# Opening of a deformable-convolution kernel: first table in quarters over six PSUM banks, last rows normalised first, patches of image 0 sent ahead of image 1's pixels

## The chip, the cores and the metric

One core of one Trainium2 chip runs the program. The metric is the device time in microseconds of one execution. The kernel before was run three times; the median is 560.41 us. The change alters only what happens in roughly the first third of the program; the rest is the same code.

## The reference, cut to what matters

The input x is 2 images of 32 channels, 64 x 64. Two residual layers follow each other, each on a group-normalised x (32 groups of one channel, so mean and variance of every channel of every image over its 4096 pixels).

```python
x = x + L0(gn(x))     # layer 0
x = x + L1(gn(x))     # layer 1

# layer 0: 3x3 convolution -> 4 offsets (dx, dy) and 4 logits per pixel
offsets = conv2d(v, offset_w, offset_b); attn = softmax(conv2d(v, weight_w, weight_b), axis=1)
sampled = grid_sample_border(v, gx + dx_n, gy + dy_n)     # 4 bilinear samples per pixel
y = conv2d(einsum('bkhwd,bkhw->bdhw', sampled, attn), proj_w)      # 1x1
y = batchnorm(y) over both images; return gelu(y)

# layer 1: 3x3 convolution -> 9 offset pairs and 9 gates, 9 bilinear samples, 3x3 output weights
```

## The kernel before, in words

All loops that concern us are in layer 0. A *group* is 512 pixels (8 image rows); each image has 8 groups, each group 4 *tiles* of 128 pixels. Layer 0 has two ways of sampling:

- **Gathers (kind "G").** Groups 0 to 4 of image 0, 20 tiles. `table00` is a DRAM table with one row of 128 floats per pixel: the 32 channels of the pixel and of its right, lower and lower right neighbour. GpSimd (POOL) issues four indirect DMAs per tile (line 565) that fetch one table row for every sample; DVE multiplies them by corner weights (line 1766, `prod`), and TensorE sums and turns the products (line 1003). There are four slots (`got`), so the gathers of tile k wait until DVE has used tile k-4 (semaphore `used`). They also wait for the whole table (`tab_out["00"]`) and for the indices of their group.
- **Windows (kind "W").** The other 11 groups, 44 tiles. `positions0` and `positions1` are DRAM copies of the raw images, pixel by pixel. A window DMA (line 490, `load_window`, two halves of 440 KB) brings 5 x 5 neighbourhoods for a group into one of two buffers in `shared`; DVE multiplies by 25 tap weights (line 1758, `samples`), TensorE sums them (line 1018). Window 0 and 1 are loaded before the loop.

The work is ordered by hand: each engine has its own list of instructions, and they meet at semaphores.

The opening. SyncE (SP) loads image 0 (four copies of the raw pixels, one for each corner shift: `x_first` for copy 0, `x_rest` for copies 1 to 3), copy 0 of image 1 and the constants `later`. DVE takes statistics; the scale and shift of each channel (`aff`) go through TensorE (line 1038) to all four partition groups. ACT and DVE normalise image 0 into `xn` by the table `SHARES` (lines 648 and 1366). TensorE makes the corner table by transposes (`make_corners`, line 926) in halves of 16 blocks, 4 corner banks each; ACT copies each bank to `trow` (line 665) and SP sends each half (line 473). `used_before` says which earlier use of a PSUM bank has to be copied away first. `make_pixels` (line 938) turns the raw pixels into patches (`prow`) for the window table; ACT copies them (line 722), SP sends them (line 479). The convolutions 0 to 15 (line 959) give offsets and logits for the items `G0, W0, G1, G2, W1, W2, G3, ...`; ACT copies each result to `conv_out` (line 677), and `turn_item` (line 996) brings it to pixel-by-row form for DVE. An item W1 needs convolution 5, W2 needs 6 and 7; from convolution 6 on image 1 is convolved.

The loop. STEPS = 20 steps m, one gather tile and two or three windows each. Tables say at which m TensorE turns an item (`TURN_AT`) and starts a convolution (`CONV_AT`), and when ACT normalises which part of image 1 (`NORM_AT`; eight pieces of 32 rows, the first before the loop). The bias of the 1x1 convolution is folded with image shifts (line 1078, y_bias line 743, `scale_fold` line 1788) before the loop, which needs `later`.

After the loop: batch statistics (line 1339), GELU, layer 1.

## Time and profile before

| | |
|---|---|
| three runs | 558.91, 560.41, 657.77 us; median 560.41 |
| profiled execution | 560.44 us, of which the span (first to last instruction) 558.6 us |
| busy share of the span | PE 83%, DVE 76%, POOL 68%, ACT 37% |
| mean granted TensorE clock | 0.90 of full speed |
| layer 0 up to the batch statistics | 0 to 168.4 us |
| layer 1 and what leads to it | 168.4 to 558.6 us |

In the rows, a time is in us from the start of the span; PE is TensorE, PEld its weight load, POOL is GpSimd, a q behind an engine marks its queue (DMA issues). In brackets stands how long the engine was idle before the row and what ended it. A TensorE instruction in 32-bit floats shows as two records (x8 for four matmuls).

### The profile page before, as it was taken

How to read it: one execution, taken by the hardware profiler on the slowest of the kernel's cores; microseconds unless marked ns; L12 is line 12 of the kernel's file. 1: busy time of each engine (PE TensorE's matmuls, PEld its weight loads, DVE VectorE, ACT ScalarE, POOL GpSimd, SP SyncE). 2: the span in 40 equal slices, each digit the busy share in tenths (PEclk: the TensorE clock that was granted, in tenths of full speed). 3: DMA queues.
4: the chain of work that ended last, by engine and by line, in shares of the span. 5: the costliest groups of instructions: out<-in, count | busy, mean ns of one | idle time of the engine just before them, and what ended most of it. 6: DMA issues, size and time to landing. Idle time of an engine off the chain costs nothing.

```text
span 558.6 us, 10900 instructions
## 1 busy us (share of the span) xinstructions
PE 464.5 (83%) x3923; PEld 263.8 (47%) x3923; DVE 422.2 (76%) x931; ACT 205.6 (37%) x342; POOL 379.2 (68%) x356
## 2 busy tenths in 40 slices
PE   5975589987870476989999999999898999998784
PEld 2545266665650332345556455555444544544443
DVE  4965529898767965678897898989788788788582
ACT  1813446322227557653433433333232332232211
POOL 5067635778744746576787777777777777777772
PEclk9855769999876576989999999999998999999999
DMA  9688443778710292111222224711112112111111
GB/s 198 192 201 198 116 93 59 162 144 137 159 30 2 76 176 61 38 62 48 73 90 73 71 91 90 102 55 53 53 48 57 53 48 58 58 53 57 54 53 30
DMA packets 42813, 48.48 MB, mean 87 GB/s; under 512 B 24454, under 2 KB 33926, under 8 KB 42000
## 3 DMA queue, kind: packets, MB, share of 16 engines
q1 hardware_dynamic: 31868, 25.52, 21.9%
q0 software_dynamic: 10752, 22.04, 14.8%
q8 instruction: 34, 0.56, 0.4%
q10 hardware_dynamic: 144, 0.24, 0.2%
q14 instruction: 15, 0.12, 0.1%
HBM read 39.02 MB, written 8.75 MB: 86 GB/s over the span
## 4 chain that ended last, share of the span: by engine, by line
PE 35%; POOL 25%; issue 15%; DMA 9%; DVE 7%; ACT 7%; SPq 1%; POOLq 1%; DVEq 0%; ACTq 0%
POOL got L565 23%; PE ps_later L1157 4%; PE ps_pair L1157 4%; PE ps_raw L1133 4%; PE ps_x L1170 4%; DMA shared<-positions 3%; ACT xn L648 3%; DMA got<-table,idx 3%; DVE samples L1758 2%; PE ps_x L1018 2%; PE ps_x L1180 2%; PE ps_raw L959 2%; PE ps_raw L1045 2%; PE ps_o L972 2%; DMA positions<-prow 2%
## 5 line engine op out<-in xcount | busy, mean ns | idle before, releaser
L565 POOL DMA_INDIRECT got<-table,idx x336 | 352.7, 1050 | 152.3 <-issue 106.9
L1775 DVE TENSOR_TENSOR prod<-got,wgt 128x512 f32<-128x512 f32 x64 | 44.3, 692 | 31.8 <-DMA got<-table,idx 31.2
L1576 DVE TENSOR_TENSOR vprod<-ps_pair,rhat 128x704 f32<-128x704 f32 x64 | 56.8, 887 | 9.2 <-PE ps_pair L1157 8.8
L1576 DVE TENSOR_TENSOR vprod<-ps_later,rhat 128x704 f32<-128x704 f32 x64 | 56.4, 882 | 1.9 <-PE ps_later L1157 1.9
L1758 DVE TENSOR_TENSOR samples<-shared,vprod 128x800 f32<-128x800 f32 x44 | 42.9, 981 | 18.4 <-DMA shared<-positions 8.7
L1170 PE MATMUL ps_x<-early,vprod 128*128 128x128 f32 x384 | 55.7, 281 | 0.8 <-DVE vprod L1584 0.5
L1170 PEld LDWEIGHTS ps_x<-early,vprod 128*128 128x128 f32 x384 | 41.9, 144 | 30.1 <-issue 16.1
L1584 DVE TENSOR_TENSOR vprod<-vprod 128x640 f32<-128x640 f32 x64 | 52.8, 824 | 1.2
L648 ACT ACTIVATE xn<-raw,aff 32x2048 f32<-32x2048 f32 (+4 forms) x20 | 42.6, 2139 | 12.5 <-DVE aff L1358 11.1
L1180 PE MATMUL ps_x<-early,prod 128*128 128x128 f32 x256 | 39.1, 275 | 9.5 <-DVE prod L1775 9.3
L1133 PE MATMUL ps_raw<-conv_out,later 128*128 128x512 f32 x64 | 40.6, 720 | 0.7 <-ACT shared L812 0.7
L798 ACT ACTIVATE samples<-ps_x 128x384 f32<-128x384 f32 x32 | 15.7, 490 | 63.4 <-PE ps_x L1180 60.3
L1018 PE MATMUL ps_x<-early,samples 128*128 128x128 f32 (+1 forms) x168 | 26.9, 320 | 13.0 <-DVE samples L1758 13.0
L1157 PE MATMUL ps_later<-y,shared 64*64 64x352 f32 x320 | 34.5, 503 | 1.9 <-DVE vprod L1576 0.7
L1157 PE MATMUL ps_pair<-y,shared 64*64 64x352 f32 x320 | 33.4, 488 | 2.6 <-DVE vprod L1576 1.5
L1180 PEld LDWEIGHTS ps_x<-early,prod 128*128 128x128 f32 x256 | 29.3, 141 | 12.2 <-DVE prod L1775 11.9
L1157 PE MATMUL ps_later<-y 64*64 64x352 f32 x320 | 32.8, 480 | 2.3 <-DVE vprod L1576 1.6
L1157 PE MATMUL ps_pair<-y 64*64 64x352 f32 x320 | 33.2, 486 | 1.7 <-DVE vprod L1576 0.9
L798 ACT ACTIVATE shared<-ps_x 128x384 f32<-128x384 f32 x32 | 15.7, 490 | 49.8 <-PE ps_x L1180 46.6
L1018 PEld LDWEIGHTS ps_x<-early,samples 128*128 128x128 f32 (+1 forms) x168 | 22.5, 160 | 19.7 <-issue 11.9
L910 PE MATMUL ps_pair<-early,xn 128*128 128x128 f32 x34 | 7.4, 399 | 22.9 <-POOL xn L550 22.9
L1576 DVE TENSOR_TENSOR vlast<-ps_later,rhat 128x704 f32<-128x704 f32 x16 | 14.3, 891 | 16.0 <-PE ps_later L1157 15.8
(200 smaller groups left out, 785.1 us busy)
## 6 DMA issues: line engine op xcount, KB each, us to landing
shared<-positions SPq DMA_DIRECT2D x22, 440.0 KB, 7.8
got<-table,idx POOLq DMA_INDIRECT x336, 5.7
raw<-in_x SPq DMA_DIRECT2D x16, 256.0 KB, 7.6
table<-trow SPq DMA_DIRECT2D x16, 256.0 KB, 2.0
y<-table SPq DMA_DIRECT2D x4, 512.0 KB, 7.9
table<-trow SPq DMA_DIRECT2D x2, 1008.0 KB
out<-ysumT SPq DMA_DIRECT2D x64, 16.0 KB
later<-in_later SPq DMA_DIRECT2D x1, 530.0 KB, 12.7
```

Of the source, the lines that this page charges most:

```text
L565: pool.indirect_dma_start(into[t][:, s * P:(s + 1) * P], None, tab, bass.IndirectOffsetOnAxis(ap=idx[:, slot, k:k + 1], axis=0),).then_inc ...
L648: nc.scalar.activation(shifted_view(b, g, r0, r1), raw_view(b, g, r0, r1), ACT.Identity, bias=aff[C * g:C * (g + 1), b, 1:2], scale=aff[C ...
L798: nc.scalar.activation(samples[u][:, :, t * P:(t + 1) * P], ps_x[t % 2][:, 0:BLOCKS1 * P].rearrange("p (k n) -> p k n", k=BLOCKS1), ACT.Co ...
L1018: last = nc.tensor.matmul(window_bank[i % 2][0:m, t * P:(t + 1) * P], wprod[t % 2][:, a:a + m], idn[:], start=(q == 0), stop=(q == len(cut ...
L1133: last = nc.tensor.matmul(ps_raw[:, :], spr[:, k, :], conv_out[g % 2][:], start=True, stop=True)
L1157: nc.tensor.matmul(ps_dense[n % 2][W * r:W * (r + 1), h * GPIX:h * GPIX + WROWS * C], chat[g % 2][W * h:W * (h + 1), pair, slot * P + W * ...
L1170: nc.tensor.matmul(bank[:, P:2 * P], vprod[:, t % 2, r, :], idn[:], start=(r == 0), stop=(r == HALF - 1), is_transpose=True)
L1180: last = nc.tensor.matmul(bank[:, 0:P], prod[:, t % 2, q * P:(q + 1) * P], idn[:], start=(q == 0), stop=(q == CORNERS - 1), is_transpose=True)
L1576: nc.vector.tensor_tensor(dst, ps_dense[pair_number(0, t, pair) % 2][:].rearrange("p (d n) -> p d n", d=2)[:, :, 0:WROWS * C].rearrange("p ...
L1584: nc.vector.tensor_tensor(vprod[:, t % 2, 0:half, :], vprod[:, t % 2, 0:half, :], vprod[:, t % 2, HALF:WROWS, :], ALU.add).then_inc(v_adde ...
L1758: nc.vector.tensor_tensor(wprod[t % 2].rearrange("p (y x c) -> p y x c", y=SIDE, c=C), window[n // TT % 2][:, :, 2 * t * C:(2 * t + SIDE) ...
L1775: nc.vector.tensor_tensor(prod[:, t % 2, :].rearrange("p (k s c) -> p s k c", k=CORNERS, c=C), got[t].rearrange("p (s k c) -> p s k c", s= ...
```

## The change

1. The corner table is made, copied and sent in four `QUARTERS` of 8 blocks instead of two `HALVES` of 16. Corner banks go round six PSUM banks instead of the hand-written list.
2. Convolution 0 comes before the first part of the table, and item G0 is turned right behind the first quarter. 4 + 2 instead of 6 + 5 idle matmuls (`keep_busy`) stand around the affine's TensorE step.
3. Image 0's normalisation: its rows are split at row 39 (`BOTTOM`). After the top 10 rows, the bottom rows come first, then the middle; ACT has copy 0 alone, DVE copies 1 to 3. The pixels of copies 1 to 3 have one semaphore for each half of the image and are loaded top half first. DVE computes the coordinates and indices of G0 between the bottom and the middle rows, and takes the statistics of image 1 behind them.
4. SP sends the patches of image 0 (`send_pixels(0)`) and loads window 0 before copies 1 to 3 of image 1's pixels; window 1 and `later` come behind them.
5. Patches of image 1 are made from copy 0 alone in two halves (`make_pixels1`), the second in step 0. The bias fold moves into step 1 (`FOLD_AT`). Image 1 is normalised in thirds (18, 23 and 23 rows) by a new `NORM_AT`: the first third, four pieces, before the loop, the rest in steps 1, 2, 4 and 5.
6. `TURN_AT` and `CONV_AT` have two slots per step: slot 0 behind the first window, slot 1 behind the gather tile.

```diff
-SHARED = 46
+BOTTOM = 39
+THIRDS = (0, 18, 41, H)
-TURN_AT = {1: [("W", 1)], 2: [("W", 2)], 3: [("G", 3)], 5: [("W", 3)], 7: [("G", 4)], 8: [("W", 4)], 11: [("W", 5)]}
-CONV_AT = {0: [5], 1: [6, 7], 2: [8], 3: [9], 4: [10], 5: [11], 6: [12], 7: [13], 8: [14], 9: [15]}
+TURN_AT = {(1, 0): [("W", 1)], (2, 0): [("W", 2)], (3, 1): [("G", 3)], (5, 0): [("W", 3)], (7, 0): [("G", 4)],
+           (8, 1): [("W", 4)], (11, 0): [("W", 5)]}
+CONV_AT = {(0, 0): [5], (1, 0): [6], (1, 1): [7], (2, 0): [8], (3, 1): [9], (4, 1): [10], (5, 1): [11], (6, 1): [12],
+           (7, 1): [13], (9, 1): [14], (10, 1): [15]}
-NORM_AT = {0: (1, 2), 1: (2, 4), 2: (4, 6), 3: (6, 8)}
+NORM_AT = {1: (4, 6), 2: (6, 8), 4: (8, 10), 5: (10, 12)}
+NORM_FOR = {6: 1, 9: 2, 13: 3}
...
-        used_before = (None, None, None, None, None, None, 0, 1, 2, 3, 6, 7, 8, 9, 10, 11)
+        corner_bank = [ps_tab[0], ps_tab[1], ps_x[0], ps_x[1], ps_o, ps_x[2]]
+        ps_first = [corner_bank[c % len(corner_bank)][:, 0:GPIX // 2] for c in range((len(QUARTERS) + 1) * CORNERS)]
+        used_before = [None] * len(corner_bank) + list(range((len(QUARTERS) + 1) * CORNERS - len(corner_bank)))
...
-        SHARES = {(0, 0): {"act": [(0, HEAD, H), (2, SHARED, H)], "pool": [],
-                           "dve": [(g, 0, HEAD) for g in range(CORNERS)] + [(1, HEAD, H), (3, HEAD, H),
-                                                                             (2, HEAD, SHARED)]},
+        SHARES = {(0, 0): {"act": [(0, BOTTOM, H), (0, HEAD, BOTTOM)], "pool": [],
+                           "dve": [(g, 0, HEAD) for g in range(CORNERS)] + [(g, BOTTOM, H) for g in (1, 2, 3)] +
+                                  [(g, HEAD, BOTTOM) for g in (1, 2, 3)]},
...
             send_corners(0, tab_copied, tab_out["00"])
-            load_rest(1)
             send_pixels(0)
             sp.wait_ge(margin_out, 64)
             sp.wait_ge(tab_out["positions0"], 16 * len(HALVES))
-            for n in range(2):
-                load_window(n)
+            load_window(0)
+            load_rest(1)
+            load_window(1)
+            sp.dma_start(later_sb[:], later).then_inc(later_in, 16)
...
             normalise(0, 0)
-            copy_corners(0, CORNERS, tab_mm, tab_copied)
             copy_conv0(0)
-            copy_corners(CORNERS, NR, tab_mm, tab_copied)
+            copy_corners(0, NR, tab_mm, tab_copied)
             exps0(ITEMS[0])
             copy_conv0(1)
-            copy_pixels(0)
+            copy_pixels0()
             copy_conv0(2)
+            copy_conv0(3)
             exps0(ITEMS[1])
-            copy_conv0(3)
+            copy_conv0(4)
             exps0(ITEMS[2])
-            copy_conv0(4)
-            copy_pixels(1)
-            act.wait_ge(y_bias_mm, 1)
-            nc.scalar.activation(y_bias[:], ps_o[:, 0:B], ACT.Copy).then_inc(y_bias_in, 1)
-            normalise(0, 1, slice(0, 1))
+            copy_pixels1(0)
+            normalise(0, 1, slice(0, CORNERS))
...
+            def make_pixels1(h):
+
+                if h:
+                    pe.wait_ge(tab_copied, NR + CORNERS + h)
+                for k, t in enumerate(HALVES[h]):
+                    last = nc.tensor.transpose(ps_o[:, k * C:(k + 1) * C],
+                                               raw[0:C, 1, t:t + BLOCKS * (P - 1) + 1:BLOCKS], idn[0:C, 0:C])
+                last.then_inc(tab_mm, 1)
...
-            keep_busy(6)
+            keep_busy(4)
             spread_affine(0)
-            keep_busy(5)
+            keep_busy(2)
+            pe.wait_ge(norm_dve, CORNERS)
+            start_conv0(0)
             for h in range(XPARTS):
                 pe.wait_ge(x_first[0][h], 16)
-            pe.wait_ge(x_rest[0], 16 * XPARTS * (CORNERS - 1))
+                pe.wait_ge(x_rest[0][h], 16 * (CORNERS - 1))
             make_corners(0, tab_copied, tab_mm, [0])
-            pe.wait_ge(norm_dve, CORNERS)
-            start_conv0(0)
-            pe.wait_ge(affine, AFFINE[0, 0])
-            make_corners(0, tab_copied, tab_mm, [1])
             turn_item(ITEMS[0])
-            normalised(0, 0)
+            make_corners(0, tab_copied, tab_mm, [1, 2, 3])
+            pe.wait_ge(norm_act, 1)
+            pe.wait_ge(norm_dve, 2 * CORNERS - 1)
             start_conv0(1)
```

How the order moves, at three places. In it, `x4` is four in a row, and a name in brackets is a semaphore that is waited for.

SP's queue from the table to the second load of patches, before:

```order
L473 DMA table<-trow 126x2048 [waits tab_copied] x2
L439 DMA raw<-in_x 32x2048 x6
L479 DMA positions<-prow 128x512 [waits tab_copied] x2
L490 DMA shared<-positions 64x5x352 [waits tab_out_positions0,margin_out]
L490 DMA shared<-positions 64x5x352 x3
L505 DMA conv_out<-in_columns 5x512 x2
L479 DMA positions<-vprod 128x512 [waits tab_copied] x2
```

and of the change:

```order
L478 DMA table<-trow 126x1024 [waits tab_copied] x4
L484 DMA positions<-prow 128x512 [waits tab_copied] x2
L495 DMA shared<-positions 64x5x352 [waits tab_out_positions0,margin_out]
L495 DMA shared<-positions 64x5x352
L445 DMA raw<-in_x 32x2048 x6
L495 DMA shared<-positions 64x5x352 x2
L509 DMA later<-in_later 128x1060
L511 DMA conv_out<-in_columns 5x512 x2
L484 DMA positions<-vprod 128x512 [waits tab_copied] x2
```

The six pixel loads of image 1 (`raw`) move behind the patches and the first window (`shared`), and `later` moves from the start to behind the second window.

TensorE from its first matmul, before (`ps_raw<-early` is `keep_busy`, `ps_o<-aff` the affine's step, L926 the table, L959 convolution 0):

```order
L1045 MATMUL ps_raw<-early 128x448 [waits early_in]
L1045 MATMUL ps_raw<-early 128x448 x5
L1038 MATMUL ps_o<-aff,early 32x2 [waits shift_in]
L1038 MATMUL ps_o<-aff,early 32x2 x3
L1045 MATMUL ps_raw<-early 128x448 x5
L926 MATMUL ps_pair<-early,raw 126x32 [waits x_rest0,x_first01,x_first00]
```

and of the change (L1069, L1062, L983 and L941 are the same four kinds):

```order
L1069 MATMUL ps_raw<-early 128x448 [waits early_in]
L1069 MATMUL ps_raw<-early 128x448 x3
L1062 MATMUL ps_o<-aff,early 32x2 [waits shift_in]
L1062 MATMUL ps_o<-aff,early 32x2 x3
L1069 MATMUL ps_raw<-early 128x448 x2
L983 MATMUL ps_raw<-xn,early 32x512 [waits norm_dve]
L983 MATMUL ps_raw<-xn,early 32x512 x2
L983 MATMUL ps_raw<-xn,early 27x512
L941 MATMUL ps_pair<-early,raw 126x32 [waits x_first01,x_rest01,x_rest00,x_first00]
```

The affine's step stands behind four idle matmuls instead of six, and convolution 0 ahead of the table.

ACT around the start of the loop, before (`prow` and `vprod` are the patches, `xn` is normalisation, `conv_out` a convolution's copy):

```order
L677 ACTIVATE conv_out<-ps_raw,early 123x512 [waits conv_mm,conv_raw]
L722 ACTIVATE vprod<-ps_x 128x256 [waits tab_mm] x2
L722 ACTIVATE vprod<-ps_pair 128x256 [waits tab_mm] x2
L743 ACTIVATE y_bias<-ps_o 128x2 [waits y_bias_mm]
L648 ACTIVATE xn<-raw,aff 32x32x64 [waits affine,pads_zero]
L682 ACTIVATE mod<-shifted 128x16 [waits logit]
L648 ACTIVATE xn<-raw,aff 32x32x64 [waits x_rest1,affine,pads_zero]
L677 ACTIVATE conv_out<-ps_raw,early 123x512 [waits conv_mm,conv_raw]
L706 ACTIVATE wshift<-wshift 128x16 [waits logit]
L687 ACTIVATE ysumT<-ps_x 128x512 [waits win_summed]
```

and of the change:

```order
L683 ACTIVATE conv_out<-ps_raw,early 123x512 [waits conv_mm,conv_raw]
L688 ACTIVATE mod<-shifted 128x16 [waits logit]
L734 ACTIVATE vprod<-ps_o 128x512 [waits tab_mm]
L654 ACTIVATE xn<-raw,aff 32x18x64 [waits affine,pads_zero]
L654 ACTIVATE xn<-raw,aff 32x18x64 [waits x_rest11,x_rest10] x3
L683 ACTIVATE conv_out<-ps_raw,early 123x512 [waits conv_mm,conv_raw]
L688 ACTIVATE mod<-shifted 128x16 [waits logit]
L734 ACTIVATE vprod<-ps_o 128x512 [waits tab_mm]
L683 ACTIVATE conv_out<-ps_raw,early 123x512 [waits conv_mm,conv_raw]
L712 ACTIVATE wshift<-wshift 128x16 [waits logit]
L693 ACTIVATE ysumT<-ps_x 128x512 [waits win_summed]
```

Four pieces of 18 rows stand ahead of the copy of convolution 5 instead of one of 32 rows and another inside step 0; y_bias moves behind the first sums.

## Rows read from the trace of the kernel before

**Rows 1.** Busy time by stage; columns: stretch, length, five engines' busy time, clock, DMA share
```profile
49.10:90.00 40.90, 31.38 (x171) 21.23 (x172) 22.45 (x68) 19.29 (x18) 21.17 (x20) 0.71 0.51 111
90.00:154.00 64.00, 53.86 (x380) 38.68 (x378) 55.07 (x128) 20.07 (x36) 50.55 (x44) 0.97 0.78 144
...
168.40:558.60 390.20, 334.74 (x3013) 175.89 (x3013) 305.14 (x639) 143.27 (x254) 279.45 (x266) 0.93 0.25 64
```

**Rows 2.** GpSimd in order of time: start, us, line, operation, idle before and releaser
```profile
30.97 1.12 POOL L565 DMA_INDIRECT got<-table,idx  x1 [19.77 <-DMA table<-trow]
...
35.91 0.59 POOL L559 TENSOR_TENSOR aff<-mv,power 32x1 f32<-32x1 f32 x1
...
79.28 0.95 POOL L565 DMA_INDIRECT got<-table,idx  x1 [7.21 <-DVE prod L1766]
...
89.03 1.41 POOL L565 DMA_INDIRECT got<-table,idx  x1 [5.01 <-DVE prod L1766]
...
96.28 0.95 POOL L565 DMA_INDIRECT got<-table,idx  x1 [0.66 <-issue]
...
159.57 1.17 POOL L565 DMA_INDIRECT got<-table,idx  x1 [0.30 <-issue]
```

**Rows 3.** DVE in order of time: the affine, and where it waited in the loop
```profile
11.23 0.15 DVE L1348 SCALAR_TENSOR_TENSOR aff<-mv,aff 32x1 f32<-32x1 f32 x1 [0.76 <-POOL aff L559]
13.47 0.16 DVE L1358 COPY aff<-ps_o 128x2 f32<-128x2 f32 x1 [2.09 <-PE ps_o L1038]
...
49.09 0.99 DVE L1758 TENSOR_TENSOR samples<-shared,vprod 128x800 f32<-128x800 f32 x1 [4.79 <-DMA shared<-positions]
...
58.63 0.17 DVE L1688 TENSOR_REDUCE wsoft<-ps_later 128x4 f32<-128x16 f32 x1 [3.74 <-PE ps_later L996]
...
83.69 0.18 DVE L1715 TENSOR_REDUCE wsoft<-wshift 128x8 f32<-128x32 f32 x1 [4.66 <-ACT wshift L706]
```

**Rows 4.** SP's DMA issues in order of time, 21 to 43 us
```profile
21.34 3.49 SPq L473 DMA_DIRECT2D table<-trow  x2
24.88 4.66 SPq L439 DMA_DIRECT2D raw<-in_x  x6
29.58 0.91 SPq L479 DMA_DIRECT2D positions<-prow  x2
38.84 4.05 SPq L490 DMA_DIRECT2D shared<-positions  x4
```

**Rows 5.** TensorE in order of time, opening and step 1
```profile
5.95 7.28 PE L1045 MATMUL ps_raw<-early 128*128 128x448 f32 x12 [5.95 <-DMA early<-in_early]
13.16 0.24 PE L1038 MATMUL ps_o<-aff,early 32*32 32x2 f32 x8
13.33 4.03 PE L1045 MATMUL ps_raw<-early 128*128 128x448 f32 x10
...
19.15 1.06 PE L959 MATMUL ps_raw<-xn,early 128*32 128x512 f32 x8
...
65.12 1.93 PE L959 MATMUL ps_raw<-xn,early 128*32 128x512 f32 x8 [3.47 <-ACT xn L648]
...
71.27 3.43 PE L996 MATMUL ps_later<-early,conv_out 123*128 123x12 f32 x16
```

**Rows 6.** ACT in order of time
```profile
13.75 4.65 ACT L648 ACTIVATE xn<-raw,aff 32x3456 f32<-32x3456 f32 x2 [11.07 <-DVE aff L1358]
...
25.78 0.66 ACT L722 ACTIVATE prow<-ps_x 128x256 f32<-128x256 f32 x2 [0.22 <-PE ps_pair L938]
...
56.73 0.69 ACT L677 ACTIVATE conv_out<-ps_raw,early 123x512 f32<-123x512 f32 x1 [0.54 <-PE ps_raw L959]
...
78.61 4.22 ACT L648 ACTIVATE xn<-raw,aff 32x2048 f32<-32x2048 f32 x2
```

**Rows 7.** DMA by stretch, columns as in rows 1 and GB/s at the end
```profile
21.30:30.97 9.67, 9.64 (x116) 6.96 (x112) 9.00 (x28) 5.46 (x13) 0.00 (x1) 0.67 0.88 274
...
38.80:49.10 10.30, 3.61 (x46) 3.24 (x42) 4.93 (x24) 4.06 (x8) 7.86 (x9) 0.50 0.68 145
```

144 lines of the change are left out of this document (81 added, 63 removed).

## The prediction

> **What bounds the kernel now.** I read the stages first [rows 1]. Layer 1 and what leads to it take 390.2 us of the 558.6 us span and the change leaves their code alone, so the question is when the batch statistics of layer 0 can start, now 168.4 us. The reader is to see that the stages of layer 0 differ: from 49.1 to 90 us DVE is busy for only 22.45 of 40.9 us and GpSimd for 21.17, while from 90 to 154 us DVE has 55.07 and GpSimd 50.55 of 64. So something waits in the middle and little waits later.
>
> Then GpSimd in order of time [rows 2]. It starts its first gather at 30.97, when the table has landed. From 96.28, the first gather of tile 9, to 159.57, the last of 80, it issues 44 gathers with no long wait: (159.57 - 96.28) / 43 = 1.47 us each. The gap between issues (0.30 us) is its own. Ahead of that it was held up twice, 7.21 us until 79.28 and 5.01 us until 89.03, both times by DVE's `prod` (slots not yet used). What follows tile 9 is a chain of fixed pace: the end of layer 0 moves as the start of that run moves. Four gathers without a wait take 35.91 - 30.97 = 4.94 us, 1.24 each, so on its own GpSimd would have been at tile 9 long before.
>
> Then DVE's waits [rows 3]: the first window is multiplied at 49.09, after 4.79 us for its DMA; 3.74 us until 58.63 for TensorE's turning of W1; 4.66 us until 83.69 for ACT's exponentials of W2. SP's queue explains the first [rows 4]: table until 24.83, six loads of image 1's pixels from 24.88 (4.66 us to issue), and only at 29.58 the patches of image 0; these are down at 38.84, when window 0 is issued, and it is there at 49.09. TensorE and ACT explain the rest [rows 5, 6]: convolution 6 at 65.12 waited 3.47 us for ACT's `xn`, convolution 5 was copied at 56.73 behind a piece of normalisation, and the exponentials of W2 stood behind 4.22 us of `xn` that began at 78.61.
>
> **The table.** TensorE's twelve records of six idle matmuls last from 5.95 to 13.23 [rows 5]; the shift was ready at 11.23 + 0.15 = 11.38 [rows 3]. With eight records they end between 5.95 + 7.28 x 8/12 = 10.8 and, if the later records are as short as the next ten (4.03 / 10 = 0.40), 13.23 - 1.6 = 11.6. The step and its copy then come at about 11.8 instead of 13.47: 1.7 us earlier. Four head pieces of 0.6 us on DVE (the first of the 7 lasts 0.60 there) end at 14.3; convolution 0, 1.06 us, at 15.4. A quarter of the table is half of what TensorE did between 17.36 and 19.15, 0.9 us: 16.3. ACT has 54 rows of copy 0; its 4.65 us from 13.75 are for 72 rows, so 3.5 us, until 15.4, and 0.7 us for convolution 0's copy. Then four copies of 256 columns per quarter; two such take 0.66 us [rows 6], 1.2 us a quarter: sent at 17.5. G0's turning (1.06 us) lies beside these copies. The second quarter runs 17.5 to 18.4, copied by 19.6; the third needs the second's first banks: 19.0 to 19.9, copied by 21.1; the last is copied by 22.6. Before, the second half was issued last in 21.34 to 24.83, at about 24.5.
>
> The transfer: 2.0 MB from 21.34 to 30.97, 9.6 us. At 0.3 MB per us (274 GB/s over the stretch with its slow start [rows 7]) it moves for 6.7 us, so 2.9 us are start and completion. The last quarter, 0.5 MB: 22.6 + 1.7 + 2.9 = 27.2. So GpSimd starts at 27.2, 3.8 us earlier. Bounds: 0 (the order gives nothing) to 5 us. Quarters speak for a loss if each paid the 2.9 us in turn. The trace has DMA busy for 0.88 of the stretch that holds both halves, so a transfer's start and end lie beside the next one's data. The Trainium skill, "DMA: Bandwidth & Descriptors", section "Rules for kernel authors", asks for 1 MiB or more per DMA, and its "Anatomy of one DMA" section for a fixed 2 us in each; by that, two more DMAs would cost 4 us. No row here shows transfers in a chain.
>
> **Patches and the first window.** They no longer wait for six pixel loads. TensorE makes them behind convolution 1 (until 22.5) and ACT copies them by about 24.8. They land at 24.8 + 1.7 + 2.9 = 29.4 instead of 38.84. Window 0 took at most 49.09 - 38.84 = 10.25 us beside window 1; now it is alone: 39.6 or earlier. Next in line is DVE itself. Its second affine waits for GpSimd's inverse, which stands behind four gathers: 27.2 + 4.94 + 0.6 = 32.7, was 36.5. From there DVE had 7.8 us of work until 49.09 - 4.79 = 44.3 [rows 3], of which 0.5 us (fold) go to step 1: about 40.4. The start of the loop moves by 49.09 - 40.4 = **8.7 us**. Three middle pieces of image 0 and five more statistics on DVE end by 28.5, covered by the wait for the inverse; convolution 3 needs them only then.
>
> **Inside the loop.** ACT has four pieces of 18 rows (1.2 us each, by 4.22 us for two of 32 rows) from about 42.7, when the first half of image 1's patches is copied, to 47.5; convolution 5 is copied by 48.3 and W1 turned by 50.2, against 58.63: the 8.7 us hold nearly in full. Queued behind the four pieces are this copy, and DVE's W1 behind it. Convolution 6 finds its rows done: the 3.47 us at 65.12 go. The `xn` block ahead of W2's exponentials shrinks from 64 rows (4.22 us) to 46 (3.0 us): 1.2 us. TensorE keeps the rest; two convolutions at half clock (1.93 us each, against 1.06 at 19.15) and turning W2 (3.43 us) stay [rows 5]. New are two blocks of 3.0 us on ACT in steps 4 and 5. Between 90 and 154 us ACT is busy for 20.07 of 64 us [rows 1], so I cost them 0.5 us; 0 if hidden, 3 if one holds up an exponential for DVE. The fold in step 1 makes TensorE wait for `later` and ACT's y_bias; behind it stands convolution 7. `later` is issued behind window 1, near 37 us, and took its turn in time if DMA moves 4 MB between 29 and 53 us, 165 GB/s; the stretch from 38.8 to 49.1 shows 145 at a share of 0.68 [rows 7], so 213 when full. Cost 0, at most 3 us.
>
> **Sum.** 8.7 + 3.5 + 1.2 - 0.5 = 12.9 us earlier at tile 8 (89.03 to about 76). GpSimd alone could be there at 27.2 + 0.6 + 32 x 1.24 to 1.47, that is 67.5 to 74.8, so DVE still sets it. The run of fixed pace then starts 12.9 us earlier. The end of it and the tail to 168.4 keep their length. 560.44 - 12.9 = **547.5 us**. The profiled execution lies 0.03 us from the median of 560.41, so this holds for both.
>
> **Rivals.** *Only the start is kept:* DVE's waits in the middle come back in another form (ACT's thirds, the fold, windows late), so the 3.5 and 1.2 us are lost. For it: TensorE was granted half its clock from 38.8 to 49.1 us, 1.2 GHz [rows 7], and window 2 now has to wait behind `later` and image 1's patches in one queue. Against it: the 3.47 us had one cause, and it is removed. 560.4 - 8.7 = 551.7, and with 3 us of new waits 554.7.
> *GpSimd is the bound all the way:* DVE's stalls shrink further, since TensorE has convolution 5 to 8 one slot earlier. Tile 9 then starts at 27.2 + 0.6 + 36 x 1.35 = 76.4 rather than 96.28: 19.9 earlier, 18 with one short wait; 542. Against it: all of TensorE's work in steps 1 to 3 is still there.
> *Quarters pay in turn:* the table is ready at 27.2 + 3 x 2.9 = 35.9, 5 later than now. The inverse, DVE and the loop follow: 40.4 + 8.7 = 49.1, the old start; 3.47 + 1.2 remain, 556. By the skill's 2 us each, an estimate from that page, it would be some 33 and 553.
> *Slower:* image 1's copies 1 to 3 now come behind window 0, and ACT's second piece waits for them, with convolution 5's copy, W1 and every DVE step queued behind. They must move 0.9 + 1.5 MB beside the gathers from 29.4. At 145 GB/s that is 16.5 us: 46. To give all back they must land 12.9 us later than the 43 that ACT could use, at 56; at half that rate (33 us) they land at 62, +6 us more: 566, and 572 if window 1, `later` and image 1's patches are late by as much again. The skill's page, section "Issuing engines are not separate DMA queues", says that SP's and GpSimd's DMAs interleave on the same 16 engines. It bears on this rival. The trace shows gathers and loads in one stretch, at a share of 0.68.
>
> **Numbers.** Forecast, with its own range of 543 to 552: 0.62. Only the start: 0.17. GpSimd the bound: 0.10. Quarters in turn: 0.05. Slower: 0.06, nearly all of it beyond the bound. A measurement of this kernel can tell about 2% from no change, 11.2 us: 549.2 and 571.6. Below 549.2 lie 0.46 of the forecast's 0.62 and the 0.10 and a little of the rest: 0.57 faster. Slower by over 2%: 0.05. The rest, 0.38, is within 2%. The range of 541 to 557 leaves out the slower case, the very end of GpSimd's and the worst of the start's.
>
> **What would show it.** In the profile of the change: first gather near 27.2; patches issued near 24.5 and window 0 near 29.5; first `samples` on DVE near 40.4 with no wait for a DMA; W1's step near 50; convolution 6 without a wait for `xn`; the first gather of tile 8 near 76 and the batch statistics near 155.5; the rest, 390.2 us, the same within 1 us. It is wrong if DVE waits for window 0 at 45 or later, if ACT's first third waits for pixels past 47, if GpSimd's pace in the long run is not 1.47 us, or if the time before the statistics shrinks and layer 1 grows.

## The result and the profile after

The changed kernel takes 551.47 us (median of 16 runs) against 559.38 for the kernel before (16 runs); the ratio is 0.9879 with a 95% interval of 0.985 to 0.9909. That is 1.2% faster. The ratio leaves out the executions that were more than 1.5% above the fastest of the same kernel (657.77 us before and 840.13 after among them), so it is not the quotient of the two medians. The forecast of 547.5 us was 4 us too low; the time lies inside the range of 541 to 557 and close to what the rival "only the start is kept" gave (551.7). As will be seen, that is not what happened: less of the start was kept than either said, and more was gained in the middle. The profiled execution took 552.87 us (span 551.0).

The stages of the changed kernel, in the stretches of [rows 1], and its layer 1 at the end:

```profile
49.10:90.00 40.90, 34.80 (x223) 24.38 (x216) 25.89 (x78) 24.75 (x30) 26.24 (x24) 0.83 0.70 144
90.00:154.00 64.00, 54.42 (x363) 39.34 (x362) 55.59 (x125) 17.25 (x31) 49.38 (x42) 0.93 0.72 135
...
161.70:551.00 389.30, 334.67 (x3013) 176.07 (x3013) 305.21 (x639) 143.15 (x254) 278.99 (x266) 0.93 0.27 64
```

The batch statistics start at 161.70 instead of 168.4, 6.7 us earlier; what follows takes 389.30 us instead of 390.20. So the gain is in layer 0, as it should be, and it is about half of the 12.9 us that the sum gave. The stretch from 49.1 to 90 us is fuller on every engine (GpSimd 26.24 for 21.17 us), and TensorE's granted clock is 0.83 there instead of 0.71.

GpSimd in order of time, to be held against [rows 2]:

```profile
28.32 1.12 POOL L570 DMA_INDIRECT got<-table,idx  x1 [17.06 <-DMA table<-trow]
...
34.68 0.56 POOL L564 TENSOR_TENSOR aff<-mv,power 32x1 f32<-32x1 f32 x1 [1.47 <-DVE mv L1376]
...
60.44 1.85 POOL L570 DMA_INDIRECT got<-table,idx  x1 [3.36 <-DVE prod L1802]
...
80.81 1.40 POOL L570 DMA_INDIRECT got<-table,idx  x1 [3.60 <-issue]
94.64 1.49 POOL L570 DMA_INDIRECT got<-table,idx  x1 [2.16 <-DVE prod L1802]
...
153.78 0.99 POOL L570 DMA_INDIRECT got<-table,idx  x1 [0.30 <-issue]
```

The first gather comes at 28.32 instead of 30.97, the first of tile 8 at 80.81 instead of 89.03, the last at 153.78 instead of 159.57. Two rows are new in kind. At 34.68 the inverse waits 1.47 us for VectorE's variance, where before it had only its own gathers ahead of it (35.91, no wait). And at 94.64, inside the run that the prediction called one of fixed pace, GpSimd waits 2.16 us.

VectorE at the start and in the loop, to be held against [rows 3]:

```profile
11.80 0.16 DVE L1394 COPY aff<-ps_o 128x2 f32<-128x2 f32 x1 [0.36 <-PE ps_o L1062]
12.00 8.42 DVE L1402 TENSOR_SCALAR xn<-raw,aff 32x640 f32<-32x640 f32 x7
...
22.50 6.67 DVE L1402 TENSOR_SCALAR xn<-raw,aff 32x1856 f32<-32x1856 f32 x3
29.20 4.83 DVE L1829 BATCH_NORM_STATS2 stats<-raw 32x6 f32<-32x512 f32 x8
...
37.31 0.14 DVE L1384 SCALAR_TENSOR_TENSOR aff<-mv,aff 32x1 f32<-32x1 f32 x1
...
44.63 0.99 DVE L1794 TENSOR_TENSOR samples<-shared,vprod 128x800 f32<-128x800 f32 x1
...
57.35 0.17 DVE L1724 TENSOR_REDUCE wsoft<-ps_later 128x4 f32<-128x16 f32 x1 [4.78 <-PE ps_later L1020]
...
75.46 0.19 DVE L1751 TENSOR_REDUCE wsoft<-wshift 128x8 f32<-128x32 f32 x1 [3.24 <-ACT wshift L712]
```

From 12.00 to 44.63 us VectorE has no gap to speak of: it is the path. The wait for window 0 (4.79 us before) is gone and the first `samples` come at 44.63 instead of 49.09. At W1's step, 57.35 for 58.63, only 1.3 us are left of this. At W2's step, 75.46 for 83.69, it is 8.2 us.

What lies between 44.63 and 57.35 is told by SyncE and ScalarE:

```profile
17.90 6.06 SPq L478 DMA_DIRECT2D table<-trow  x4
26.25 1.62 SPq L484 DMA_DIRECT2D positions<-prow  x2
29.66 1.34 SPq L495 DMA_DIRECT2D shared<-positions  x2
31.04 7.76 SPq L445 DMA_DIRECT2D raw<-in_x  x6
```

```profile
47.26 1.34 ACT L654 ACTIVATE xn<-raw,aff 32x1152 f32<-32x1152 f32 x1
51.33 4.09 ACT L654 ACTIVATE xn<-raw,aff 32x1152 f32<-32x1152 f32 x3 [2.73 <-DMA raw<-in_x]
55.45 0.69 ACT L683 ACTIVATE conv_out<-ps_raw,early 123x512 f32<-123x512 f32 x1
```

Patches 0 are issued at 26.25 and window 0 follows at 29.66 (38.84 before). But image 1's pixels now come behind window 0, and ScalarE's second piece waits 2.73 us for them; convolution 5's copy and W1's step are queued behind.

What lies between W1's step and W2's is told by TensorE, to be held against the last three lines of [rows 5]. First the stretch before and after, with the granted clock in the third column from the end, then the changed kernel's convolutions 6 and 7 and its turning of W2:

```profile
60.00:76.00 16.00, 11.67 (x57) 7.66 (x58) 7.33 (x27) 6.27 (x6) 8.22 (x8) 0.57 0.42 99
60.00:76.00 16.00, 13.81 (x96) 9.84 (x94) 9.53 (x34) 9.74 (x12) 11.72 (x11) 0.87 0.74 151
```

```profile
57.24 1.77 PE L983 MATMUL ps_raw<-xn,early 128*32 128x512 f32 x8
...
61.90 1.06 PE L983 MATMUL ps_raw<-xn,early 128*32 128x512 f32 x8 [0.31 <-issue]
...
63.71 0.96 PE L1020 MATMUL ps_later<-early,conv_out 123*128 123x12 f32 x8
65.73 1.06 PE L1020 MATMUL ps_later<-early,conv_out 123*128 123x12 f32 x8 [1.06 <-ACT conv_out L683]
```

Convolution 6 has no wait for `xn` any more (3.47 us before), and TensorE does these steps at a higher granted clock: 0.87 of full speed from 60 to 76 us instead of 0.57.

### The profile page after: what moved, and what is told of

The parts are those of the page before. It is cut to its first block, busy times and chain, and to the rows that moved or that the text cites. A ratio compares the mean times of both kernels' runs of the same rounds, so it can differ in the third digit from the quotient of the medians.

```text
span 551.0 us, 10909 instructions
## 1 busy us (share of the span) xinstructions
PE 459.4 (83%) x3913; PEld 261.4 (47%) x3913; DVE 429.5 (78%) x934; ACT 206.5 (37%) x352; POOL 379.0 (69%) x356
## 4 chain that ended last, share of the span: by engine, by line
PE 35%; POOL 25%; issue 15%; DVE 8%; DMA 8%; ACT 6%; SPq 1%; POOLq 1%; DVEq 0%; ACTq 0%
POOL got L570 23%; PE ps_later L1193 4%; PE ps_pair L1193 4%; DMA got<-table,idx 4%; PE ps_x L1206 4%; PE ps_raw L1169 4%; ACT xn L654 3%; DMA raw<-in_x 3%; PE ps_raw L983 3%; PE ps_x L1216 2%; PE ps_o L996 2%; POOL xn L555 1%; PE ps_pair L1042 1%; PE ps_later L1020 1%; SPq L445 1%
## 5 line engine op out<-in xcount | busy, mean ns | idle before, releaser
L1612 DVE TENSOR_TENSOR vprod<-ps_later,rhat 128x704 f32<-128x704 f32 x64 | 56.5, 882 | 0.9 <-PE ps_later L1193 0.8
L1206 PEld LDWEIGHTS ps_x<-early,vprod 128*128 128x128 f32 x384 | 42.4, 145 | 30.6 <-issue 17.3
L654 ACT ACTIVATE xn<-raw,aff 32x1472 f32<-32x1472 f32 (+6 forms) x24 | 43.0, 1802 | 13.6 <-DVE aff L1394 9.4
L1193 PE MATMUL ps_pair<-y,shared 64*64 64x352 f32 x320 | 34.6, 504 | 2.1 <-DVE vprod L1612 1.0
L1042 PEld LDWEIGHTS ps_x<-early,samples 128*128 128x128 f32 (+1 forms) x168 | 21.3, 154 | 16.3 <-DVE samples L1794 8.4
L1020 PE MATMUL ps_later<-early,conv_out 123*128 123x12 f32 x128 | 17.7, 272 | 10.9 <-DVE vprod L1739 6.4
```

The source lines that it names most:

```text
L654: nc.scalar.activation(shifted_view(b, g, r0, r1), raw_view(b, g, r0, r1), ACT.Identity, bias=aff[C * g:C * (g + 1), b, 1:2], scale=aff[C ...
L1042: last = nc.tensor.matmul(window_bank[i % 2][0:m, t * P:(t + 1) * P], wprod[t % 2][:, a:a + m], idn[:], start=(q == 0), stop=(q == len(cut ...
L1193: nc.tensor.matmul(ps_dense[n % 2][W * r:W * (r + 1), h * GPIX:h * GPIX + WROWS * C], chat[g % 2][W * h:W * (h + 1), pair, slot * P + W * ...
L1206: nc.tensor.matmul(bank[:, P:2 * P], vprod[:, t % 2, r, :], idn[:], start=(r == 0), stop=(r == HALF - 1), is_transpose=True)
L1612: nc.vector.tensor_tensor(dst, ps_dense[pair_number(0, t, pair) % 2][:].rearrange("p (d n) -> p d n", d=2)[:, :, 0:WROWS * C].rearrange("p ...
```

## The experiments

Twelve runs followed, of eleven kernels (one was run twice, and one is the changed kernel itself). On the two chips that they ran on, the kernel before took 713 to 724 us, not 559; the chip of the first comparison is not on record, and I call it the first chip. Both kernels are longer there, mostly in layer 1, whose code the change doesn't touch: in the profiles of these twelve runs it lasts 531 to 548 us, against 389. A difference of 2 to 4 us in the opening therefore drowns in a total, and I read these runs by when each step starts in their profiles, and by totals only where they differ by more than 1%. Up to the first `samples` the control's steps agree with the first comparison's within 0.1 us, except for its first gather, 0.7 us later. Even the start of the batch statistics decides little: with the same code (even rows, run twice) it came at 165.50 and 167.41 us, and in the other runs of the changed kernel and its variants between 166.77 and 175.36.

### Even counts of rows

```diff
-BOTTOM = 39
+BOTTOM = 38
```

> The changed kernel with BOTTOM = 38 for 39: VectorE's six pieces of image 0 are then 26 and 28 rows instead of 25 and 29, one row moved from the middle pieces to the last ones, nothing else. Theory (an odd count of rows halves VectorE's pace on this copy of rows of 64 into rows of 66): 1,664 and 1,792 elements by the 0.6 ns of the 36- and 54-row pieces of the kernel before, so 1.05 to 1.2 us each instead of 1.93 and 2.20; the six together 6.7 instead of 12.4 us, the batch affine of image 0 (37.31) then bound by GpSimd's four gathers at 33 to 34.5, the first samples at 41 to 42.5 instead of 44.63, of which what TensorE's wait for image 1's pixels leaves is kept: 547 to 550 us against 551.5 for the changed kernel. Rival (it is the shortness of the pieces, or what runs beside them): the forms stay at 1.9 to 2.3 us and the time at 551 to 552.

VectorE's forms in the changed kernel and with this one line changed (mean ns behind the busy time):

```profile
L1402 DVE TENSOR_SCALAR xn<-raw,aff 32x1856 f32<-32x1856 f32 x3 | 6.6, 2201 | 0.1
L1402 DVE TENSOR_SCALAR xn<-raw,aff 32x1600 f32<-32x1600 f32 x3 | 5.8, 1932 | 0.1
```

```profile
L1402 DVE TENSOR_SCALAR xn<-raw,aff 32x1792 f32<-32x1792 f32 x3 | 3.6, 1208 | 0.1
L1402 DVE TENSOR_SCALAR xn<-raw,aff 32x1664 f32<-32x1664 f32 x3 | 3.4, 1140 | 0.1
```

In order of time, with that line changed, VectorE and then ScalarE:

```profile
29.04 0.36 DVE L1375 BATCH_NORM_AGGREGATE mv<-stats 32x2 f32<-32x48 f32 x1
...
34.93 0.15 DVE L1384 SCALAR_TENSOR_TENSOR aff<-mv,aff 32x1 f32<-32x1 f32 x1 [2.24 <-POOL aff L564]
...
42.20 0.99 DVE L1794 TENSOR_TENSOR samples<-shared,vprod 128x800 f32<-128x800 f32 x1
```

```profile
52.48 4.11 ACT L654 ACTIVATE xn<-raw,aff 32x1152 f32<-32x1152 f32 x3 [6.17 <-issue]
```

The 26 and 28 rows take 1.14 and 1.21 us where 25 and 29 took 1.93 and 2.20. The aggregate comes 5.0 us earlier (29.04 for 34.06), though the affine copy was 0.3 us later here. Image 0's six pieces were on the path; now the affine waits 2.24 us for GpSimd, as in the kernel before, and the loop starts 2.4 us earlier. The mechanism is settled in the theory's favour: the middle pieces start at row 10 in both kernels, and only their count changed. The gain in time is not shown: the ratio is 0.9869 (0.9815 to 0.9922), and ScalarE's second piece now waits until 52.48, so that convolution 5 is copied at 56.62, later than in the changed kernel.

### An odd count in the kernel before

```diff
-SHARED = 46
+SHARED = 45
```

> The kernel before with SHARED = 45 for 46: VectorE's share of corner 2 is 35 rows (2,240 elements) instead of 36, ScalarE's 19 instead of 18. Theory (odd count of rows halves VectorE's pace): that piece takes 2.6 to 2.8 us instead of 1.47, and what follows on VectorE at the start is 1.2 us later. Rival (the count's parity does nothing; other work or the place made the changed kernel's pieces slow): 1.43 us. ScalarE's piece grows from 18 to an odd 19 rows; theory and rival alike give it 1/18 more.

The kernel before, and with 45:

```profile
L1366 DVE TENSOR_SCALAR xn<-raw,aff 32x3456 f32<-32x3456 f32 x2 | 4.2, 2075 | 0.1
...
L1366 DVE TENSOR_SCALAR xn<-raw,aff 32x2304 f32<-32x2304 f32 x1 | 1.5, 1469 | 0.0
```

```profile
L1366 DVE TENSOR_SCALAR xn<-raw,aff 32x2240 f32<-32x2240 f32 x1 | 2.6, 2596 | 0.0
```

One row fewer, and the piece takes 2.60 us instead of 1.47. This is in the kernel before, at another place and with a larger size, so neither the shortness of the pieces nor what stood beside them in the changed kernel is the cause. (This kernel was run once. Its second aggregate came 17.3 us behind the affine copy, against 15.4 in the kernel before: 1.8 us later, not 1.2.) The two rates are (2,075 - 1,469) / 1,152 = 0.53 ns per element for 54 and 36 rows, and (2,201 - 1,932) / 256 = 1.05 ns for 29 and 25. From the latter, 35 rows should take 1,932 + 640 x 1.05 = 2,604 ns: 2,596 were measured. ScalarE's pieces show no such step: 25, 26, 28 and 29 rows took 1,726, 1,776, 1,869 and 1,922 ns.

### Image 1's pixels ahead of window 0, or waited for by halves

```diff
             send_pixels(0)
+            load_rest(1)
             sp.wait_ge(margin_out, 64)
             sp.wait_ge(tab_out["positions0"], 16 * len(HALVES))
             load_window(0)
-            load_rest(1)
```

> The changed kernel with image 1's six pixel loads for corners 1 to 3 issued right behind patches 0, ahead of SyncE's wait for the patches and of window 0 (where the kernel before has them relative to window 0). Theory (the copies of image 1 wait for exactly these loads, 2.73 us, and window 0 has slack): ScalarE's second normalisation piece of image 1 no longer waits, the group of three ends by about 51.5 instead of 55.45, window 0 is issued at about 36 instead of 29.7 and lands 9 to 10 us later at 45 to 46, 1 us behind the first samples at 44.6; net 1 to 2 us faster, 549.5 to 550.5. Rival (the two transfers share the same rate, so that what the pixels gain the window loses): first product waits for window 0 for 3 us or more and the time is 551 to 553.

```profile
28.34 2.76 SPq L445 DMA_DIRECT2D raw<-in_x  x6
31.20 2.71 SPq L495 DMA_DIRECT2D shared<-positions  x4
```

```profile
47.98 5.46 ACT L654 ACTIVATE xn<-raw,aff 32x1152 f32<-32x1152 f32 x4
53.48 0.69 ACT L683 ACTIVATE conv_out<-ps_raw,early 123x512 f32<-123x512 f32 x1
```

The wait of 2.73 us is gone and convolution 5 is copied 2.0 us earlier than in the first comparison (53.48 for 55.45). A run on the same chip that leaves SyncE's order as in the changed kernel (the table in two halves, below) has the wait again and copies convolution 5 at 57.85:

```profile
53.73 4.10 ACT L654 ACTIVATE xn<-raw,aff 32x1152 f32<-32x1152 f32 x3 [2.70 <-DMA raw<-in_x]
```

So the wait was for these loads. Window 0 was issued at 31.20, not at 36 as I had expected, because the six loads took 2.76 us to issue here against 7.76 behind window 0; the first `samples`, at 45.17, did not wait for it. The ratio is 0.9841 (0.9786 to 0.9895).

The other way to take the wait away, SyncE's order left as it is:

```diff
-                        for h in range(XPARTS):
+                        for h in range(XPARTS if r1 > H // XPARTS else 1):
                             act.wait_ge(x_rest[b][h], 16 * (CORNERS - 1))
```

> The changed kernel, where ScalarE's pieces of image 1 that end above row 32 wait for the first half of the pixels alone instead of both. Theory (the 2.73 us wait is for the last landing loads of corners 1 to 3, while the first half has landed 1.3 us or more before): the wait falls to 1.4 us or less, conv 5 is copied about 1.3 us or more earlier than 55.45 and the whole is 0.5 to 1.5 us faster. Rival (the halves land together since they share the queues): the wait stays 2.5 us and the time at 551 to 552.

ScalarE's four pieces ran without a wait from 48.26 to 53.7 and convolution 5 was copied at 53.74: the first half of the pixels had landed by 49.6 at the latest. Ratio 0.9859 (0.9807 to 0.9911).

### Both, and what comes next

> The same kernel as in the first run with even rows, timed again for its interval, since there TensorE stood idle for up to 4 us at a time behind nothing that the profile shows. Theory (with even pieces VectorE is off the path and image 1's pixels are on it): the batch affine again at 34.9, the first samples at 42.2, ScalarE's second normalisation piece of image 1 waits for pixels for 4 to 6 us until about 51, conv 5 is copied at 55 to 56 as in the changed kernel, and the time is at most 1 us below the changed kernel's: ratio to the kernel before 0.984 to 0.989. Rival (the wait of the first run was that chip's; the pixels land as early as VectorE needs them): ratio 0.980 to 0.983.

Batch affine 35.06, first `samples` 42.34, ScalarE's wait 4.74 us until 51.05, convolution 5 copied at 55.17, against 55.45 in the changed kernel. Ratio 0.9881 (0.9824 to 0.9939). So the 2.3 us won at the loop's start are lost again 9 us later, as the theory had it; the releaser of that wait is not named in the trace.

Even rows and the six loads ahead of window 0:

> Even rows and image 1's six pixel loads ahead of window 0, together. Theory (two things in series held the loop: VectorE's odd pieces its start, the late pixels its second step): the first samples at 42 to 43, ScalarE's four pieces of image 1 without a wait from 45.5 to 51, conv 5 copied at 51.5 to 52.5 against 55.45, and 2.5 to 4 us less than the changed kernel: ratio to the kernel before 0.980 to 0.984. Rival (window 0, issued behind the six loads, becomes the late one): VectorE's first samples wait for it until 45 or later, and the time is that of the run with the pixels first alone, 1 us less than the changed kernel at most.

The first `samples` came at 45.43, after 1.87 us of wait, and ScalarE's pieces ran without one. But everything was 1.1 us late from the affine copy on (12.91 for 11.80), and convolution 5 was copied at 54.12, not by 52.5: ScalarE stood idle 2.53 us just before that copy, behind nothing on this core that the trace names. Neither theory alone: with VectorE in time, window 0 became the late one, as the rival said. Ratio 0.9872 (0.9822 to 0.9922). The next run, with the same opening, names what is waited for. In it ScalarE's copies go ahead of its normalisation blocks in steps 4 and 5:

```diff
-                if m in NORM_AT:
+                if m in NORM_AT and m < 4:
                     normalise(0, 1, slice(*NORM_AT[m]))
                 for n in CONV_AT.get((m, 1), []):
                     copy_conv0(n)
+                if m in NORM_AT and m >= 4:
+                    normalise(0, 1, slice(*NORM_AT[m]))
...
-NORM_FOR = {6: 1, 9: 2, 13: 3}
+NORM_FOR = {6: 1, 9: 2, 12: 3}
```

> As the run before, and in steps 4 and 5 ScalarE copies its convolution ahead of the two normalisation pieces instead of behind them (TensorE then waits for all twelve pieces before conv 12 instead of conv 13). Theory (these two blocks of 3.25 us hold the copies of convs 10 and 11, for which TensorE waits 1.60 us at 87.57 in the changed kernel): that wait goes, and the time falls by 1 to 2 us more. Rival (the copies and turns only move; what waits next is the sums' copy behind the same blocks): no wait for conv_out at that place but the same for ysumT, time within 0.5 us of the run before.

TensorE and VectorE without and with the swap (the first fence is the run before):

```profile
90.83 1.74 PE L1020 MATMUL ps_later<-early,conv_out 123*128 123x12 f32 x8 [1.60 <-ACT conv_out L683]
...
94.26 0.99 DVE L1794 TENSOR_TENSOR samples<-shared,vprod 128x800 f32<-128x800 f32 x1 [2.62 <-PE ps_pair L1042]
```

```profile
44.04 0.99 DVE L1796 TENSOR_TENSOR samples<-shared,vprod 128x800 f32<-128x800 f32 x1 [2.12 <-DMA shared<-positions]
...
95.93 1.05 DVE L1796 TENSOR_TENSOR samples<-shared,vprod 128x800 f32<-128x800 f32 x1 [2.38 <-DMA shared<-positions]
```

The same two waits stand in the changed kernel (1.60 us at 87.57, 2.27 us at 90.61) and lie behind GpSimd's 2.16 us at 94.64. The swap removes both. In their place VectorE waits 2.38 us for the next window's transfer. The next tile's product came at 100.90, against 102.08 in the run before: 56.86 and 56.65 us after their own first `samples`. One tile earlier the swap had been 3.2 us ahead by the same measure (92.40 and 96.96). Nothing of it was kept, though the next wait was not the one that the rival named. Ratio 0.9921 (0.9878 to 0.9963).

The table in two halves:

```diff
-                for q, part in enumerate(QUARTERS):
-                    sp.wait_ge(copied, CORNERS * (q + 1))
+                for q, part in enumerate(HALVES):
+                    sp.wait_ge(copied, 2 * CORNERS * (q + 1))
```

> The changed kernel with the table of image 0 sent in two halves (behind the eighth and the sixteenth copy) instead of four quarters, nothing else. Theory (sending the last quarter alone is worth what the smaller last transfer saves, since the copies end where they end): first gather 0.5 to 1.5 us later than 28.32, GpSimd's four gathers and the first samples as before or up to 1 us later since VectorE sets them, time 0 to 1 us more. Rival (the early quarters bring the whole gain of the gather): first gather 2.5 us or more later, at 31 as in the kernel before, and the time 2 us more.

The first gather came at 30.03, 17.56 us behind the affine copy at 12.47. In the changed kernel on the first chip this distance is 16.52. In the nine runs here that sent quarters it is 16.9 to 17.8 us, in the kernel before 17.50 (first comparison) and 17.48 and 16.86 (runs here). So sending quarters is worth at most 1 us, and these runs don't show that it is worth anything. The ratio, 0.9954 (0.9908 to 0.9999), is no clearer.

### The control and the last two candidates

> The changed kernel itself, for its ratio and its trace on the chip of this call. If this chip is like the first two calls' (kernel before at 713 to 716 us, the second layer slower), every theory expects the ratio to lie nearer to 1 than the 0.988 of the first comparison, since the opening's gain of about 8 us is divided by more and a part is lost in what follows: 0.986 to 0.994. On a chip like that of the first comparison (before at 559): 0.985 to 0.991. The forms of VectorE's pieces: 1.93 and 2.20 us either way.

The ratio is 0.9866 (0.9772 to 0.996): the gain of the first comparison is there on these chips too. Its profiled execution was the longest of its six (719.04 us), so I take no marks from it behind the first `samples`. Up to there they are those of the first comparison: affine 37.35 (37.31), `samples` 44.68 (44.63).

Even rows with the wait by halves:

> Even rows, and ScalarE's pieces of image 1 that end above row 32 wait for the first half of the pixels alone; SyncE's order as in the changed kernel. Theory (the pixels' first half lands by about 46 and the second by 51, window 0 stays early): first samples at 42.3 with no wait for window 0, ScalarE's four pieces of image 1 without a wait of over 1.5 us, conv 5 copied at 51.5 to 53, 2.5 to 4 us less than the control. Rival (both halves land late together, as their transfers share the rate with window 0): the wait stays 4 us or more, conv 5 at 55, within 1 us of the control.

First `samples` at 42.33 with no wait, ScalarE's pieces from 45.07 with one wait of 1.68 us, convolution 5 copied at 52.20: as the theory had it but for the wait, which it had at 1.5 us or less.

```profile
48.08 4.09 ACT L654 ACTIVATE xn<-raw,aff 32x1152 f32<-32x1152 f32 x3 [1.68 <-issue]
```

The only edit between this and the two runs of even rows is what that instruction waits for, and its wait fell from 6.17 and 4.74 us. So the wait whose releaser the trace left open was for the second half of the pixels (the runs were on different chips). But the lead was lost right behind. TensorE in this run:

```profile
53.77 0.40 PE L1020 MATMUL ps_later<-early,conv_out 123*128 123x12 f32 x2
54.69 0.39 PE L1020 MATMUL ps_later<-early,conv_out 123*128 123x12 f32 x2 [0.52 <-issue]
...
56.14 0.61 PE L1020 MATMUL ps_later<-early,conv_out 123*128 123x12 f32 x3 [0.56 <-issue]
56.89 4.07 PE L983 MATMUL ps_raw<-xn,early 128*32 128x512 f32 x8
```

The eight records of W1's turning and the eight of convolution 6 take 7.2 us (granted clock 0.64), with gaps behind nothing that the trace names, where the changed kernel on the first chip had them done in 2.7 us (56.28 to 59.0, clock 0.72). At the ninth tile's product this run stands at 106.17, the even rows alone at 105.77 and the wait by halves alone at 107.55. The time is 716.58 us against the control's 712.84, where 2.5 to 4 us less than the control had been expected; the ratio, 0.9959 (0.9918 to 0.9999), overlaps the control's.

With, in addition, the first half of the pixels ahead of window 0 (`load_rest(1, [0])` behind `send_pixels(0)`, `load_rest(1, [1])` behind window 0):

> As the run before, and the three loads of the first half of image 1's pixels are issued right behind patches 0, in SyncE's wait for the patches; window 0 and the second half follow. Theory (they use a stretch of 1.8 us in which SyncE and most of the transfer rate are free, and are 0.77 MB ahead of 0.88 MB of window 0): first half landed by 40, window 0 by 42 to 43, first samples at 42.3 to 43.3, ScalarE's pieces without a wait, conv 5 copied at 51 to 52.5; 3 to 4.5 us less than the control. Rival (window 0 is late by what the pixels take, as with all six ahead of it, where it landed at 44 to 45.4): first samples at 44 or later and nothing gained on the run before.

First `samples` at 42.42 without a wait, pieces without a wait from 46.82, convolution 5 at 52.81 (0.3 us past what was expected): this part is the theory's. The time, 716.75 us, and the ratio, 0.9943 (0.9895 to 0.9992), show no gain over the control. No version that I ran is shown to beat the changed kernel.

### One part alone

```diff
             send_corners(0, tab_copied, tab_out["00"])
-            load_rest(1)
             send_pixels(0)
...
-            for n in range(2):
-                load_window(n)
+            load_window(0)
+            load_rest(1)
+            load_window(1)
```

> One part of the change alone: the kernel before with SyncE's order of the change (patches 0, window 0, then image 1's six pixel loads, then window 1). Theory (the order pays only with TensorE's wait for image 1's corners 1 to 3 taken out of the opening, which the change also does): patches land at 28 to 29, window 0 by 40, VectorE's first samples at 43.5 to 45 instead of 49.09, but TensorE turns image 1's pixels, and with them everything behind, only when the six loads are in, at 48 to 52 instead of 38.9; statistics of the batch 0 to 4 us later than the kernel before and the ratio 1.000 to 1.007. Rival (the order alone brings the gain of the loop's start): TensorE turns image 1's pixels by 43 and the ratio is 0.990 to 0.994.

```profile
42.92 0.98 DVE L1758 TENSOR_TENSOR samples<-shared,vprod 128x800 f32<-128x800 f32 x1
...
51.66 0.32 PE L938 MATMUL ps_x<-early,raw 32*128 32x32 f32 x2 [13.97 <-issue]
```

This is the kernel before with the change's order on SyncE and nothing else, and it is slower: 1.0164 (1.0038 to 1.029). VectorE starts the first window at 42.92, as hoped, but TensorE turns image 1's pixels at 51.66 instead of 38.90. The trace names no releaser; by the code it waits there for all six loads. W1's step then comes at 64.11 instead of 58.63. The order pays only with TensorE's wait for corners 1 to 3 taken out of the opening. It cost more than I had expected (ratio up to 1.007).

## Why the prediction was right, and where it was not

The time lies in the stated range, 4 us above the forecast. It got there by errors that partly cancel: W1's step came 7.1 us later than the sum had it (57.35 for 50.2), and the middle then gave about 3 us more. The prediction gave 0.57 to more than 2% faster and 0.38 to within 2%, where the result lies.

**The affine and the table.** The affine copy at 11.80 is what the sum had. The first gather came 2.65 us earlier, not 3.8. ScalarE's last two copies ran from 22.95 for 0.67 us, so the last quarter went out at 23.6, 1 us later than forecast (22.6); its transfer then took 28.32 - 23.62 = 4.7 us, as the step had it (1.7 + 2.9 = 4.6). What was mis-sized is the taking of turns over the six banks: ScalarE stood still 0.67 to 0.77 us before each quarter but the first. Of the 2.65 us, 1.67 are the affine's (11.80 for 13.47) and 1 at most the quarters'. The rival "quarters pay in turn" is out: it had the table ready at 35.9. The fixed 2 us that it takes from the Trainium skill, "DMA: Bandwidth & Descriptors", section "Anatomy of one DMA", are given there for DMAs that GpSimd issues, while these are SyncE's. The 33 us worked out from them was not seen either: the first gather came at 28.32.

**The first window.** Patches issued at 26.25 and window 0 at 29.66 were forecast at 24.8 and 29.4. With even rows the `samples` start at 42.2 without a wait for it, so it was not the bound. Right.

**The step that failed** is "three middle pieces of image 0 and five more statistics on DVE end by 28.5, covered by the wait for the inverse". They ended at 34.03 and the inverse waited for them. The cover is gone because the six pieces take 12.4 us; the end at 28.5 leaves them 6.9, which is about the rate of the kernel before's even counts. One row moved (even rows) brings the end to 29.0 and the affine's wait for GpSimd back. Where nothing else was moved ahead of it, the loop then starts at 42.2 to 42.4: this is 2.3 of the 4.2 us by which it was late (44.63 for 40.4). The rest goes with the table, whose first gather in those runs came at 29.4 to 29.6 instead of 27.2. On the first chip it came at 28.32 and the four gathers ended at 33.2; with the 7.9 us that the run with even rows has from the inverse (34.31) to the first `samples`, the loop would have started at about 41.1, an estimate, so there the odd pieces cost some 3.5 us. The sum has a slip of its own here: 32.7 + 7.8 - 0.5 is 40.0 and not 40.4, so that its own terms give 13.3 us and 547.1.

One page bears on this: the Trainium skill, "VectorE: DVE Perf Modes", section "Mode 2×_2P — use both read ports for one tensor", lets a one-source operation take two elements per cycle if the outermost dimension is even, or odd and equal for source and destination. The trace agrees for the even counts, 0.53 ns per element against 1.05 for the odd ones. For the odd counts the rule alone does not settle it: source and destination have the same odd count of rows in the kernel. The source's rows touch and the destination's don't, so the condition would fail if touching rows are taken as one run; that is argued, and no run here isolates it. Neither the prediction nor its rivals held the new row counts against it.

**ACT's four pieces until 47.5, W1's step at 50.2.** They ended at 55.42, and W1's step came at 57.35. Of the pieces' 7.9 us, 4.2 come from the loop's start, 0.6 from the pieces themselves (5.4 us for 4.8) and 2.73 from the wait for pixels, which was the prediction's slower rival at a fraction of its price: it said 46 for the landing at full rate, and the second half landed at 51.3. That the wait is for these loads is shown by the two runs that remove it in different ways. The remark that ScalarE waiting past 47 would prove the forecast wrong held.

**The middle.** Convolution 6 has no wait for `xn` any more, and the block ahead of W2's exponentials is shorter (3.25 us for 4.22): the sum had 3.5 + 1.2 = 4.7 us. Measured by VectorE's products, the lead over the kernel before grows from 0.9 us at the third (63.12 for 64.01) to 6.8 at the fourth (71.01 for 77.81) and 8.5 at the sixth (86.29 for 94.82): 7.6 us. The two terms were right as mechanisms, 3.5 and 1.0 us. What the sum had wrong is "TensorE keeps the rest", with the two convolutions at half clock and the turning of W2 unchanged. TensorE was granted 0.87 of its clock from 60 to 76 us instead of 0.57: convolutions 6 and 7 took 1.77 + 1.06 us instead of 1.93 + 1.93 and the turning of W2 0.96 + 1.06 instead of 3.43. By these rows that is 2.4 us, an estimate, since no run changes the clock alone. The three make 6.9 of the 7.6 us. The rival "only the start is kept" was wrong in both of its halves and near the time by accident.

**The two new blocks on ACT: 0.5 us, bound 3.** The lead of VectorE's products falls from 8.5 to 6.0 us at the seventh, behind them, and is 7.8 again at the eighth. GpSimd's lead falls from 8.7 to 6.8 us at 94.64 and does not come back. So their term was about 2 us. That they hold the copies is shown (the swap removes the waits); that 2 us could be had by moving them is not, since the next window's transfer takes their place.

**The fixed pace.** 44 gathers from 87.76 to 153.78 take (66.02 - 2.16) / 43 = 1.49 us each without that wait, forecast 1.47. The fold cost nothing that a row shows. Layer 1 took 389.3 for 390.2.

The account: forecast 12.9 us at tile 8, 8.2 there and 8.5 at tile 9; less 2.2 for the wait that GpSimd meets at 94.64 and 0.6 for the slightly slower pace, 5.8 at the last gather; 0.9 regained between it and the statistics: 6.7. With 0.9 us in layer 1 it is 7.6 in the profiled span, 7.9 in the medians.

Open stays whether the even rows with the wait by halves beat the changed kernel on a chip like the first: no run on such a chip was made. Also open are what holds TensorE up on the other chips, and the 0.9 us in layer 1.

## What to carry to other kernels

Before a piece of work is cut into smaller pieces, work out each piece's shape against the rule by which the engine takes its fast mode, and price it by a row of the same parity. A cut at 39 instead of 38 cost 5 us of VectorE's time here, and the old cuts had all been even. When a queue is reordered to bring one transfer forward, list who waits for those that are pushed back: an order that pays with such a wait removed cost 1.6% without it. And a step priced as "covered" should name by how much, since here a margin of 3.6 us (28.5 against the inverse at 32.1) was eaten by one wrong rate. Last, a step priced at the clock that it had before may find another one: here 0.87 was granted from 60 to 76 us, where it had been 0.57.
